# Second attention of a four-stage transformer kernel: sixteen units of two batches, with the sum of the fused halves carried in SBUF

## The chip, the cores and the metric

The kernel runs on one core of a Trainium2 chip. The metric is the device time of one execution in microseconds (us); of several runs the median counts. The core has five engines with queues of their own: TensorE (PE, with its weight loads as PEld), VectorE (DVE), ScalarE (ACT), GpSimd (POOL) and SyncE (SP), which issues DMAs. Each runs its instructions in order and waits on semaphores for the others.

## The reference

Four blocks follow one another on x, of 16 batches, 100 tokens and 256 channels: a cross attention, a mixture of experts, a second cross attention whose linear layers are rounded to integers, and a recurrent cell. The change is in the third block:

```python
vis = bitnet_linear(dinov2_features, W_d2v, b_d2v)
image_embeds = bitnet_linear(vis, W_img, b_img)
fused = bitnet_linear(text_embeddings, W_txt, b_txt)
for Wa, ba in ((W_att0, b_att0), (W_att1, b_att1)):
    kv = bitnet_linear(image_embeds, Wa, ba)
    k = jnp.concatenate([kv, kv], axis=-1)
    scores = jnp.einsum('bse,bpe->bsp', fused, k) * inv_sqrt_e
    attn = jax.nn.softmax(scores, axis=-1)
    fused = fused + 0.1 * jnp.einsum('bsp,bpe->bse', attn, k)
avg_img = jnp.mean(image_embeds, axis=1, keepdims=True)
concatenated = jnp.concatenate([fused, jnp.broadcast_to(avg_img, (b, s, e))], axis=-1)
h = jax.nn.relu(bitnet_linear(concatenated, W_f1, b_f1))
```

`bitnet_linear` divides its input by the maximum of the whole tensor over 127, rounds it, and multiplies by weights of -1, 0 and 1. So the maximum over all of `concatenated` must be known before F1 starts. `kv` has 128 channels, and since k is kv twice, a score needs only the sum of the two 128-channel halves of `fused`. The image has 361 places (KV) in a batch.

## The kernel before

The stage lies between the text product, whose eight results ScalarE writes to `fused` (L1891), and the maximum over `fused` (L1983, L1487) on which the scale of F1 hangs. There are four passes over four batches each (Q = 4), and in each pass two layers r, so eight rounds. `att_tensor`, `att_scalar` and `att_vector` write the rounds out for each engine. TensorE does in a round, for all four batches in turn: keys (L1632) and values (L1637), scores (L1644), transposes of the probabilities (L1649), and attention by values (L1655). Each of these takes float32 operands but the first two. ScalarE evicts the keys (L1669), takes exponentials (L1673) and copies the transposed probabilities (L1677). VectorE evicts the values (L1688), adds the two halves of `fused` into `f12` (L1693), takes the negated scores with their minimum (L1696), the reciprocals (L1700) and the divisions of the probabilities (L1702), and adds a tenth of the result to both halves of `fused` (L1707). Once in a pass it takes the maximum over the four batches before (L1711).

Banks: batch q has bank q for keys, scores and result, and bank 4+q for values and transposes. A round's keys wait for the update of the round before, batch by batch. The first and last pass are written out, the other two are a loop.

Image roundings (L1586 on ScalarE, L1590 on VectorE) prepare two halves of `img_q`, one batch an instruction: all sixteen are done ahead of the attention, VectorE's odd ones while the text product runs and ScalarE's last four behind the text evictions. GpSimd adds f2's bias to x in four instructions (L1792) once the normalised x is taken; before and after that stand its reductions over partitions (L1492). Behind them it makes the cell's weights (L2161), which wait for the cell's loads (issued by SyncE after the last update) and for the scaled inputs of F1, of which VectorE's L1991 writes the last.

Of the kernel before, what the change touches and what calls it, by code (L numbers as in the profile page):

```python
# [10 lines left out]
ALU = mybir.AluOpType  # L11
ACT = mybir.ActivationFunctionType
AX = mybir.AxisListType
# [23 lines left out]
LG = 4  # L37
# [11 lines left out]
def build(nc, a, out):  # L49
    ctx = ExitStack()  # L50
    with ctx:
# [1567 lines left out]

        def att_tensor(pe):  # L1620
            def body(t, *_):
                first = isinstance(t, int) and t == 0
                for r in range(2):
                    n = 8 * t + 4 * r
                    for q in range(Q):
                        b = 4 * t + q
                        if first and r == 0 and q == 0:
                            pe.wait_ge(c_p1, B // 2 + B + B // 4)
                            pe.wait_ge(c_q, B // 2 + B // 4)
                        wait(pe, n_u, n + q - 3)  # L1630
                        for k in range(CC):
                            i = pe.matmul(bank[q][:, 0:KV], w_q[ATT + r][:, k, :],  # L1632
                                          img_q[:, k, bass.ds(b * KV, KV)], start=(k == 0), stop=(k == 1))
                        i.then_inc(n_k, 1)
                        for j in range(KJ):
                            for k in range(CC):
                                i = pe.matmul(bank[4 + q][0:KT, j * 128:(j + 1) * 128],  # L1637
                                              img_q[:, k, bass.ds(b * KV + j * KT, KT)], w_q[ATT + r][:, k, :],
                                              start=(j == 0 and k == 0), stop=(k == 1), skip_group_check=True)
                        i.then_inc(n_v, 1)  # L1640
                    for q in range(Q):
                        pe.wait_ge(n_ke, n + q + 1)
                        pe.wait_ge(n_f, n + q + 1)
                        pe.matmul(bank[q][0:T, 0:KV], f12[q], kvT[q], start=True, stop=True).then_inc(n_s, 1)  # L1644
                    for q in range(Q):
                        pe.wait_ge(n_ve, n + q + 1)
                        pe.wait_ge(n_p, n + q + 1)
                        for j in range(KJ):
                            i = pe.transpose(bank[4 + q][0:KT, j * T:(j + 1) * T],  # L1649
                                             prob[q][:, j * KT:(j + 1) * KT], ident[0:T, 0:T])  # L1650
                        i.then_inc(n_t, 1)
                    for q in range(Q):
                        pe.wait_ge(n_pte, n + q + 1)
                        for j in range(KJ):
                            i = pe.matmul(bank[q][:, 0:T], kvt[q][:, j, :], probT[q][:, j, :],  # L1655
                                          start=(j == 0), stop=(j == KJ - 1))
                        i.then_inc(n_o, 1)
                if first:
                    pe.wait_ge(c_p1, 2 * B)
                    pe.wait_ge(c_q, B)  # L1660
            run(pe, B // Q, 1, 0, 1, body)

        def att_scalar(s):
            def body(t, *_):
                for r in range(2):
                    n = 8 * t + 4 * r
                    for q in range(Q):
                        s.wait_ge(n_k, n + q + 1)
# [978 lines left out]
```

## Time and profile before

| | |
|---|---|
| median of 3 runs | 997.46 us (996.68 to 1001.53) |
| profiled execution | 992.82 us, of which the span of the core is 991.0 us |
| PE busy | 821.7 us (83%) |
| DVE busy | 725.7 us (73%) |
| ACT busy | 556.1 us (56%) |
| POOL busy | 292.6 us (30%) |
| chain that ended last, by engine | PE 54%, DVE 24%, issue 8%, ACT 7% |
| second attention | 745.5 to 854.6 us of the span |

The profile is a record of one execution. Its timeline lists instructions with start and duration, merged where the same instruction repeats; its groups give the number, the busy time and the mean of one; what stands in brackets or behind the last bar is the idle time of the engine just before, and what ended it. A matmul's recorded duration contains the drain of the array, so in a row of matmuls the starts tell the pace. PEclk is the clock granted to TensorE, 1.00 for 2.4 GHz and 0.50 for 1.2 GHz.

### The profile page before, as it was taken

The page shows a single profiled execution, that of the slowest core. Times are in us where ns is not written, and L with a number is a line of the kernel's source. Part 1 is how long each engine was busy: PE and PEld are TensorE (multiplying, and loading weights), DVE is VectorE, ACT ScalarE, POOL GpSimd, SP SyncE. Part 2 cuts the span into 40 slices and gives each one's busy share as a digit, 9 for nine tenths or more (in the row PEclk, how much of TensorE's full clock was granted, in tenths as well). Part 3 has the DMA queues.
Part 4 walks back from the last instruction along what each step waited for, and adds up shares of the span by engine and source line. Part 5 has one row for each costly group of instructions (what it writes and reads, how often), then busy time and mean ns, then how long its engine had stood idle before and what let it go on. Part 6 is the DMA issues. An engine that isn't in the chain of part 4 may idle for free.

```text
span 991.0 us, 22346 instructions
## 1 busy us (share of the span) xinstructions
PE 821.7 (83%) x8198; PEld 604.3 (61%) x8198; DVE 725.7 (73%) x1496; ACT 556.1 (56%) x1147; POOL 292.6 (30%) x238
## 2 busy tenths in 40 slices
PE   3777888988898777798899999986647888769995
PEld 2345666666666554587666777772125777549994
DVE  7568787787877898767566776636995666776865
ACT  3446666666665436433555556538975555573542
POOL 3336444353441515040421110007603000053400
PEclk9978999999999777999999999995557888889998
DMA  6423443334453346323275555534200000200002
GB/s 182 106 67 75 97 105 91 100 105 111 121 115 81 82 167 225 110 57 115 74 200 163 163 166 167 142 102 120 71 10 0 2 0 0 85 0 2 3 1 67
DMA packets 76991, 90.47 MB, mean 91 GB/s; under 512 B 22166, under 2 KB 64945, under 8 KB 76842
## 3 DMA queue, kind: packets, MB, share of 16 engines
q1 hardware_dynamic: 69562, 80.95, 29.6%
q0 software_dynamic: 6144, 7.42, 2.8%
q10 hardware_dynamic: 1216, 1.18, 0.4%
q8 instruction: 43, 0.70, 0.3%
q14 instruction: 26, 0.21, 0.1%
HBM read 73.86 MB, written 15.43 MB: 90 GB/s over the span
## 4 chain that ended last, share of the span: by engine, by line
PE 54%; DVE 24%; issue 8%; ACT 7%; DMA 3%; POOL 2%; SPq 1%; ACTq 0%; DVEq 0%; POOLq 0%
PE ps L1151 11%; PE ps L1138 8%; PE ps L337 4%; PE ps L527 4%; PE ps L425 3%; PE ps L1655 3%; PE ps L499 3%; DVE p L515 3%; PE ps L569 3%; DVE m L485 2%; PE ps L2099 2%; PE ps L480 2%; PE ps L1649 2%; PE ps L2110 1%; DVE pmax L1616 1%
## 5 line engine op out<-in xcount | busy, mean ns | idle before, releaser
L485 DVE TENSOR_REDUCE m<-ps 100x2 f32<-100x722 f32 x128 | 115.2, 903 | 52.9 <-PE ps L480 51.3
L506 ACT ACTIVATE p<-ps 128x800 f32<-128x800 f32 x128 | 106.8, 835 | 43.0 <-PE ps L499 40.0
L1200 ACT ACTIVATE hT<-ps,cols 128x500 f32<-128x500 f32 (+1 forms) x96 | 62.5, 651 | 106.4 <-PE ps L1138 98.3
L1151 PE MATMUL ps<-w_h,hT_h 128*125 128x256 f16 (+1 forms) x384 | 105.9, 276 | 7.4 <-DVE x L1247 6.8
L515 DVE SCALAR_TENSOR_TENSOR p<-p 128x600 f32<-128x600 f32 x128 | 107.0, 838 | 0.0
L1207 DVE TENSOR_TENSOR hT_l<-hT,hT_h 128x500 f16<-128x500 f32 (+1 forms) x96 | 62.3, 652 | 60.9 <-ACT hT_h L1201 60.9
L1151 PE MATMUL ps<-w_h,hT_l 128*125 128x256 f16 (+1 forms) x384 | 105.9, 276 | 0.0
L1151 PE MATMUL ps<-w_l,hT_h 128*125 128x256 f16 (+1 forms) x384 | 105.8, 276 | 0.0
L1043 POOL DMA_INDIRECT xe<-tokens,slot_of x32 | 43.1, 1347 | 155.4 <-PE ps L1161 102.1
L1138 PE MATMUL ps<-xe_h,w_h 128*128 128x500 f16 (+1 forms) x192 | 71.7, 374 | 14.3 <-ACT hT_h L1201 6.1
L499 PE MATMUL ps<-qs,ks 128*128 128x100 f16 x768 | 64.7, 215 | 14.3 <-ACT p L506 14.3
L1138 PE MATMUL ps<-xe_l,w_h 128*128 128x500 f16 (+1 forms) x192 | 71.2, 371 | 0.0
L1138 PE MATMUL ps<-xe_h,w_l 128*128 128x500 f16 (+1 forms) x192 | 71.0, 370 | 0.0
L499 PEld LDWEIGHTS ps<-qs,ks 128*128 128x128 f16 x768 | 52.5, 101 | 28.5 <-ACT p L506 20.0
L355 POOL TENSOR_TENSOR kp<-k,kp 128x361 f16<-128x361 f32 x32 | 31.3, 977 | 118.5 <-ACT kp L351 118.5
L480 PE MATMUL ps<-ks,qs 128*100 128x361 f16 x256 | 63.0, 332 | 1.6 <-DVE xnT L168 1.4
L1201 ACT ACTIVATE hT_h<-ps,cols 128x500 f16<-128x500 f32 (+1 forms) x96 | 62.1, 647 | 0.0
L1492 POOL PARTITION_ALL_REDUCE gmax<-cmax x6 | 2.2, 365 | 196.4 <-DVE cmax L1487 190.5
L1151 PEld LDWEIGHTS ps<-w_h,hT_h 128*125 128x125 f16 (+1 forms) x384 | 51.5, 134 | 12.3 <-DVE x L1247 6.0
L527 PE MATMUL ps<-p,v 128*32 128x100 f32 (+1 forms) x1536 | 48.0, 259 | 8.8 <-DVE p L515 8.6
L1151 PEld LDWEIGHTS ps<-w_l,hT_h 128*125 128x125 f16 (+1 forms) x384 | 51.6, 134 | 2.6
L1151 PEld LDWEIGHTS ps<-w_h,hT_l 128*125 128x125 f16 (+1 forms) x384 | 51.6, 134 | 0.0
(342 smaller groups left out, 2209.4 us busy)
## 6 DMA issues: line engine op xcount, KB each, us to landing
sw<-in_L_ffn_w_dram SPq DMA_DIRECT2D x16, 512.0 KB, 6.3
sw<-in_L_ffn_w_dram SPq DMA_DIRECT2D x8, 1024.0 KB, 5.9
k_parts<-kp SPq DMA_DIRECT2D x32, 192.0 KB, 2.0
ks<-k_parts SPq DMA_DIRECT2D x32, 192.0 KB
stage<-in_L_xattn_W_f_dram SPq DMA_DIRECT2D x6, 1024.0 KB, 7.4
ctx_f<-in_ctxT_dram SPq DMA_DIRECT2D x16, 270.8 KB, 3.1
stage<-in_ctxT_dram SPq DMA_DIRECT2D x8, 541.5 KB, 8.6
area<-in_ctxT_dram SPq DMA_DIRECT2D x16, 270.8 KB, 6.2
```

What stands on the lines that cost most here:

```text
L480: mm = pe.matmul(bank[at + n][0:T, 0:KV], qs[p][:, h, :], ks[p][:, h, 0:KV], start=True, stop=True)
L485: v.tensor_reduce(m32[p][:, 2 * i:2 * i + 2], ps[0:T, at:at + 2, 0:KV], AX.X, ALU.max).then_inc(m_max, 1)
L499: mm = pe.matmul(bank[t_bank(i) + n][:, j * T:(j + 1) * T], keys, qs[p][:, h, :], start=(j == 0), stop=True, skip_group_check=True)
L506: s.activation(p32[:, i % HALF, :, :, :].rearrange("p j n t -> p n j t"), ps[:, t_bank(i):t_bank(i) + 2, 0:(KJ + 1) * T].rearrange("p n (j ...
L515: v.scalar_tensor_tensor(probs, probs, 1.0, low, ALU.min, ALU.max).then_inc(a_cv, 1)
L527: i = pe.matmul(OB_[HR * r:HR * (r + 1), g * T:(g + 1) * T], v32[p][0:m, j, h, :], p32[0:m, h // 2 % HALF, j, h % 2, :], start=(g == 0 and ...
L1043: g.indirect_dma_start(xe[e % 2][:, j, :], None, x_d, bass.IndirectOffsetOnAxis(ap=slot_of[:, 4 * e + j:4 * e + j + 1], axis=0)).then_inc( ...
L1138: i = pe.matmul(bank[2 + f % 2][:, 0:width(n)], w1p[ww][:, k, f * 128:(f + 1) * 128], xep[p][xx][:, k, 0:width(n)], start=(k == 0 and ww = ...
L1151: i = pe.matmul(bank[4 + j % 3][0:m, 0:C], hTp[p][hh][:, f, j * m:(j + 1) * m], w2p[of][ww][:, f, :], start=(f == 0 and hh == ww), stop=(f ...
L1200: s.activation(hT[:, f % 3, 0:m], bank[2 + f % 2][:, 0:m], ACT.Silu, bias=bias, scale=1.0 / WS)
L1201: s.activation(hTp[p][0][:, f, 0:m], bank[2 + f % 2][:, 0:m], ACT.Silu, bias=bias, scale=1.0 / WS).then_inc(f_s, 1)
L1207: v.tensor_tensor(hTp[p][1][:, f, 0:m], hT[:, f % 3, 0:m], hTp[p][0][:, f, 0:m], ALU.subtract).then_inc(f_l, 1)
```

## The change

The eight rounds of four batches become sixteen units of two. Unit u belongs to a pair of batches and a layer: the units 0 to 3 are pair 0 layer 0, pair 1 layer 0, pair 0 layer 1, pair 1 layer 1, and so on with the next pairs. On TensorE the work of three units is interleaved: scores of u, result of u-1, values and keys of u+1, transposes of u. Keys and scores have banks 0 and 1, values 2 and 3, transposes 4 and 5, results 6 or 7 by turns, two batches in one. All units are written out, without a loop.

`f12` covers two batches. GpSimd adds the halves of `fused` for it (new function `att_gpsimd`), once for each pair; for the second layer VectorE adds two tenths of the first layer's result to it straight from PSUM, beside the update of `fused`. The four additions of f2's bias now stand behind every second of these additions. The image roundings of the batches 5 and up on VectorE, and 8 and up on ScalarE, are put behind given units. The maximum over `fused` is taken in three parts of four batches, one of two before the last update and one of two after; the one over the image's mean comes ahead of the attention.

```diff
-        f12 = [over_vis(128, T) for _ in range(Q)]
+        f12 = [over_vis(128, 2 * T) for _ in range(2)]
+        UNITS = B
+        ROUND_ACT = {2: 8, 4: 10, 6: 12, 8: 14}
+        ROUND_DVE = {0: 5, 1: 7, 3: 9, 4: 11, 6: 13, 8: 15}
...
+            keys_values(0)
+            for u in range(UNITS):
+                if unit_of(u)[1] == 0:
+                    pe.wait_ge(n_f, u // 4 * 2 + u % 2 + 1)
+                else:
+                    pe.wait_ge(n_u, u - 1)
+                for q in range(2):
+                    pe.wait_ge(n_ke, 2 * u + q + 1)
+                    pe.matmul(bank[q][0:T, 0:KV], f12[u % 2][:, q * T:(q + 1) * T], kvT[at_slot(u, q)],
+                              start=True, stop=True).then_inc(n_s, 1)
+                values_out(u - 1)
+                keys_values(u + 1)
+                for q in range(2):
+                    pe.wait_ge(n_p, 2 * u + q + 1)
+                    for j in range(KJ):
+                        i = pe.transpose(bank[4 + q][0:KT, j * T:(j + 1) * T],
+                                         prob[at_slot(u, q)][:, j * KT:(j + 1) * KT], ident[0:T, 0:T])
+                    i.then_inc(n_t, 1)
+            values_out(UNITS - 1)
...
+            for u in range(UNITS):
+                for q in range(2):
+                    at = at_slot(u, q)
+                    s.wait_ge(n_sc, 2 * u + q + 1)
+                    s.activation(prob[at][:, 0:KV], neg_s[at], ACT.Exp, scale=-1.0, bias=small[:, 0, at:at + 1],
+                                 accum_out=small[:, 1, at:at + 1]).then_inc(n_e, 1)
+                keys(u + 1)
...
+                if u in ROUND_ACT:
+                    round_scalar(s, IMG_, img_f, img_q, 128, ROUND_ACT[u])
...
+        def att_gpsimd(g):
+
+            g.wait_ge(h_ev, 8)
+            for pair in range(B // 2):
+                tok = pair_tokens(pair)
+                u = pair // 2 * 4 + pair % 2
+                wait(g, n_s, 2 * (u - 1))
+                g.tensor_tensor(f12[u % 2], fused[:, 0, tok], fused[:, 1, tok], ALU.add).then_inc(n_f, 1)
+                if pair % 2:
+                    x_b2_gpsimd(g, pair // 2)
...
+                v.wait_ge(n_o, u + 1)
+                if unit_of(u)[1] == 0:
+                    v.scalar_tensor_tensor(f12[u % 2], bank[6 + u % 2][:, 0:2 * T], 0.2, f12[u % 2], ALU.mult, ALU.add)
+                v.scalar_tensor_tensor(fused[:, :, tok], bank[6 + u % 2][:, None, 0:2 * T].broadcast_to((128, CC, 2 * T)),
+                                       0.1, fused[:, :, tok], ALU.mult, ALU.add).then_inc(n_u, 1)
...
+                normalise(u, 0)
+                update(u - 1)
+                normalise(u, 1)
+                values(u + 1)
+                if u in ROUND_DVE:
+                    round_vector(v, IMG_, img_f, img_q, 128, ROUND_DVE[u])
+                if u % 4 == 1 and u > 4:
+                    v.wait_ge(n_u, u - 1)
+                    fused_max(u // 4 - 1, u // 4 * 4 - 4, u // 4 * 4)
+            v.wait_ge(n_u, UNITS - 1)
+            fused_max(3, B - 4, B - 2)
+            update(UNITS - 1)
+            v.wait_ge(n_u, UNITS)
+            vs.inc(fused_max(5, B - 2, B))
```

TensorE before, the first round (area3 holds the rounded image, area2 all of the attention's tiles; L1632 keys, L1637 values, L1644 scores, L1649 transposes, L1655 result):

```order
L1632 MATMUL ps<-area3,wq_att0 128x361 [waits c_q,c_p1,h_ev]
L1632 MATMUL ps<-area3,wq_att0 128x361
L1637 MATMUL ps<-wq_att0,area3 121x128 x6
L1632 MATMUL ps<-area3,wq_att0 128x361 x2
...
L1644 MATMUL ps<-area2 100x361 [waits n_f,n_ke] x4
L1649 MATMUL ps<-const,area2 121x100 [waits n_p,n_ve]
L1649 MATMUL ps<-const,area2 121x100 x2
...
L1655 MATMUL ps<-area2 128x100 [waits n_pte]
L1655 MATMUL ps<-area2 128x100 x2
```

TensorE now, unit 1 (L1680 scores, L1667 result of unit 0, L1647 values and L1655 keys of unit 2, L1687 transposes):

```order
L1680 MATMUL ps<-area2 100x361 [waits n_ke,n_f]
L1680 MATMUL ps<-area2 100x361 [waits n_ke]
L1667 MATMUL ps<-area2 128x100 [waits n_pte,n_ve]
L1667 MATMUL ps<-area2 128x100 x2
...
L1647 MATMUL ps<-wq_att1,area3 121x128 [waits n_ve]
L1647 MATMUL ps<-wq_att1,area3 121x128 x5
...
L1655 MATMUL ps<-area3,wq_att1 128x361 [waits n_sc]
L1655 MATMUL ps<-area3,wq_att1 128x361
...
L1687 MATMUL ps<-const,area2 121x100 [waits n_p]
L1687 MATMUL ps<-const,area2 121x100 x2
```

Between scores and transposes there was nothing; now the result of one unit and the keys and values of another stand there.

VectorE before, the second round of the first pass (L1688 values, L1693 sum of the halves, L1696 negated scores, L1700 and L1702 reciprocal and division, L1707 update):

```order
L1688 SCALAR_TENSOR_TENSOR area2<-ps,oscale,att_b1 121x384 [waits n_v]
L1693 TENSOR_TENSOR area2<-fused 128x100 [waits n_u]
...
L1696 TENSOR_SCALAR area2<-ps 100x361 [waits n_s] x4
L1700 RECIPROCAL area2<-area2 100x1 [waits n_e]
L1702 TENSOR_SCALAR area2<-area2 100x361 [waits n_r]
...
L1707 SCALAR_TENSOR_TENSOR fused<-ps,fused 128x2x100 [waits n_o] x4
```

VectorE now, unit 5 and the start of what follows (L1768 negated scores, L1744 and L1746 reciprocal and division, L1755 the carried sum, L1756 update, L1735 values of the next unit):

```order
L1768 TENSOR_SCALAR area2<-ps 100x361 [waits n_s] x2
L1744 RECIPROCAL area2<-area2 100x1 [waits n_e]
L1746 TENSOR_SCALAR area2<-area2 100x361 [waits n_r]
L1755 SCALAR_TENSOR_TENSOR area2<-ps,area2 128x200 [waits n_o]
L1756 SCALAR_TENSOR_TENSOR fused<-ps,fused 128x2x200
L1744 RECIPROCAL area2<-area2 100x1 [waits n_e]
L1746 TENSOR_SCALAR area2<-area2 100x361 [waits n_r]
L1735 SCALAR_TENSOR_TENSOR area2<-ps,oscale,att_b1 121x384 [waits n_v] x2
```

The update of the unit before stands between the two divisions, and the value evictions behind them.

GpSimd before, between the reduction for the text's scale and the one for F1's:

```order
L1492 ISA gmax<-cmax 128x1 [waits q_max] x2
L1792 ISA
L1792 TENSOR_TENSOR x<-x,f_b 100x1024 [waits ln_xn,c_b_in]
L1792 TENSOR_TENSOR x<-x,f_b 100x1024 x3
L1492 ISA
L1492 ISA gmax<-cmax 128x1 [waits q_max]
```

and now (L1724 sum of the halves, L1862 f2's bias):

```order
L1496 ISA gmax<-cmax 128x1 [waits q_max] x2
L1724 ISA
L1724 TENSOR_TENSOR area<-fused 128x200 [waits h_ev]
L1724 TENSOR_TENSOR area<-fused 128x200
L1862 TENSOR_TENSOR x<-x,f_b 100x1024 [waits ln_xn,c_b_in]
L1724 TENSOR_TENSOR area<-fused 128x200 [waits n_s] x2
L1862 TENSOR_TENSOR x<-x,f_b 100x1024
L1724 TENSOR_TENSOR area<-fused 128x200 [waits n_s] x2
L1862 TENSOR_TENSOR x<-x,f_b 100x1024
```

The additions of the bias are no longer in one row: each is released by the scores that its neighbour L1724 waits for.

## Rows read from the trace of the kernel before

**Rows 1.** Busy time by stretch: whole stage, and a piece of it; PEclk granted.

```profile
core 0: us, PE busy (x) PEld busy (x) DVE busy (x) ACT busy (x) POOL busy (x), PEclk, DMA share, GB/s
745.50:854.60 109.10, 93.51 (x608) 75.19 (x608) 73.77 (x227) 61.36 (x137) 9.17 (x4) 0.86 0.00 0
...
757.20:765.00 7.80, 7.73 (x37) 7.74 (x38) 2.47 (x8) 2.14 (x6) 0.00 (x0) 0.50 0.00 0
```

**Rows 2.** Groups of the stage: busy us, mean ns of one | idle before, releaser.

```profile
L1688 DVE SCALAR_TENSOR_TENSOR area<-ps,oscale,att_b 121x384 f32<-121x384 f32 x32 | 19.6, 612 | 6.8 <-PE ps L1637 6.8
...
L1707 DVE SCALAR_TENSOR_TENSOR fused<-ps,fused 128x200 f32 (+1 forms) x32 | 11.7, 366 | 29.4 <-PE ps L1655 29.4
...
L1673 ACT ACTIVATION_READ_ACCUMULATOR area<-area 100x1 f32 x32 | 6.0, 186 | 0.0
...
L1711 DVE TENSOR_REDUCE pmax<-fused x3 | 2.9, 974 | 0.0
```

**Rows 3.** Timeline of a round at full clock: start us, duration us, engine, instruction.

```profile
791.38 0.47 PE L1632 MATMUL ps<-area,wq_att 128*128 x2
...
793.96 2.63 PE L1644 MATMUL ps<-area 128*100 128x361 f32 x8
...
795.55 0.53 DVE L1696 TENSOR_SCALAR_CACHE_REDUCE area<-ps 100x361 f32<-100x361 f32 x1
...
796.12 0.60 ACT L1673 ACTIVATE area<-area 100x361 f32<-100x361 f32 x1 [1.64 <-DVE area L1696]
...
797.36 0.16 DVE L1700 RECIPROCAL area<-area 100x1 f32<-100x1 f32 x1
797.55 0.41 DVE L1702 TENSOR_SCALAR area<-area 100x361 f32<-100x361 f32 x1
...
798.11 2.07 PE L1649 MATMUL ps<-const,area 100*121 100x100 f32 x12 [1.51 <-DVE area L1702]
...
798.68 1.95 ACT L1677 COPY area<-ps 121x300 f32<-121x300 f32 x4
...
800.02 2.84 PE L1655 MATMUL ps<-area 121*128 121x100 f32 x24
...
800.89 0.37 DVE L1707 SCALAR_TENSOR_TENSOR fused<-ps,fused 128x200 f32 x1 [1.39 <-PE ps L1655]
...
802.70 0.47 PE L1632 MATMUL ps<-area,wq_att 128*128 x2
```

**Rows 4.** Timeline: first keys of two rounds that follow one another.

```profile
764.92 0.81 PE L1632 MATMUL ps<-area,wq_att 128*128 128x361 f16 x2
...
779.84 0.81 PE L1632 MATMUL ps<-area,wq_att 128*128 x2
```

**Rows 5.** Timeline of the front of the stage, all engines.

```profile
739.68 3.12 DVE L1590 TENSOR_SCALAR area<-area,iinv 128x722 f16<-128x722 f32 x6
...
745.33 9.35 POOL L1792 TENSOR_TENSOR x<-x,f_b 100x1024 f32<-100x1024 f32 x4 [7.22 <-issue]
745.45 3.27 ACT L1586 ACTIVATE area<-area,iinv 128x722 f16<-128x722 f32 x4
...
745.62 0.48 PE L1632 MATMUL ps<-area,wq_att 128*128 128x361 f16 x2 [1.32 <-ACT fused L1891]
...
748.26 1.88 DVE L1693 TENSOR_TENSOR area<-fused 128x100 f32<-128x100 f32 x1
748.73 1.28 ACT L1669 ACT_TABLE_LOAD   x1
...
750.74 1.46 PE L1644 MATMUL ps<-area 128*100 128x361 f32 x4 [2.36 <-ACT area L1669]
```

**Rows 6.** Timeline behind the stage: what GpSimd's weights wait for, and they.

```profile
860.01 0.76 DVE L1991 TENSOR_SCALAR area<-avg,iinv 128x400 f16<-128x400 f32 x2
...
865.41 5.91 POOL L2161 TENSOR_SCALAR fused<-area 128x512 f16<-128x512 f32 x4 [9.00 <-issue]
```

**Rows 7.** Timeline: end of the stage, the maximum over all parts.

```profile
855.73 0.16 DVE L1487 TENSOR_REDUCE cmax<-pmax 128x1 f32<-128x5 f32 x1
```

**Rows 8.** Timeline of an earlier stretch: a cast beside GpSimd's additions.

```profile
370.73 15.40 POOL L1262 TENSOR_TENSOR x<-x,pick_more 100x1024 f32<-100x1024 f32 x4 [20.02 <-DVE pick_more L1349]
...
379.19 2.35 DVE L1056 CAST upper<-const 100x100 bf16<-100x100 f32 x1
```

More of the change, by code:

```diff
@@ L1617, in lin_max_vector @@
                             ).then_inc(c_pm, 1)
-        def att_tensor(pe):
[L1621 to L1630, printed above, removed]
-                        for k in range(CC):
[L1632 to L1661, printed above, removed]
@@ L1663, in att_scalar @@
-        def att_scalar(s):
[L1664 to L1668, printed above, removed]
-                        s.activation(kvT[q], bank[q][:, 0:KV], ACT.Identity, scale=oscale[:, ATT + r:ATT + r + 1],
-                                     bias=col(f"L1_xattn_b_att{r}")).then_inc(n_ke, 1)
-                    for q in range(Q):
-                        s.wait_ge(n_sc, n + q + 1)
-                        s.activation(prob[q][:, 0:KV], neg_s[q], ACT.Exp, scale=-1.0, bias=small[:, 0, q:q + 1],
-                                     accum_out=small[:, 1, q:q + 1]).then_inc(n_e, 1)
-                    for q in range(Q):
-                        s.wait_ge(n_t, n + q + 1)
-                        s.copy(probT[q], bank[4 + q][0:KT, 0:KJ * T].rearrange("p (j t) -> p j t", j=KJ)
-                               ).then_inc(n_pte, 1)
-            run(s, B // Q, 0, 0, 1, body)
@@ new lines, in att_scalar, with keys @@
+        def att_scalar(s):
+            def keys(u):
+                if u == UNITS:
+                    return
+                r = unit_of(u)[1]
+                for q in range(2):
+                    s.wait_ge(n_k, 2 * u + q + 1)
+                    s.activation(kvT[at_slot(u, q)], bank[q][:, 0:KV], ACT.Identity,
+                                 scale=oscale[:, ATT + r:ATT + r + 1], bias=col(f"L1_xattn_b_att{r}")).then_inc(n_ke, 1)
+            keys(0)
+            for u in range(UNITS):
+                for q in range(2):
+                    at = at_slot(u, q)
[3 more added lines that the diff above has]
+                keys(u + 1)
+                for q in range(2):
+                    s.wait_ge(n_t, 2 * u + q + 1)
+                    s.copy(probT[at_slot(u, q)], bank[4 + q][0:KT, 0:KJ * T].rearrange("p (j t) -> p j t", j=KJ)
+                           ).then_inc(n_pte, 1)
+                if u in ROUND_ACT:
+                    round_scalar(s, IMG_, img_f, img_q, 128, ROUND_ACT[u])
@@ L1784, in y2_vector, with x_b2_gpsimd @@
                                        oscale[0:T, F2:F2 + 1], x[:, b:b + 2, :], ALU.mult, ALU.add).then_inc(y_ev, 2)
[L1786 to L1792 removed]
+        def x_b2_gpsimd(g, n):
+            if n == 0:
+                g.wait_ge(c_b_in, 48)
+                g.wait_ge(ln_xn, 3 * B)
+            part = x[:, LB * n:LB * (n + 1), :]
+            g.tensor_tensor(part, part, f2_b[:, None, :].broadcast_to((T, LB, C)), ALU.add).then_inc(x_bias, 1)
         def last_stats(v, g):
@@ L1893, in layer2_scalar @@
                              ).then_inc(h_ev, 1)
-            for b in range(B // 2, B, 2):
-                round_scalar(s, IMG_, img_f, img_q, 128, b)
             s.wait_ge(pad_set, 1)
@@ L1971, in layer2_vector @@
                                 ).then_inc(h_q2, 1)
-            for b in range(5, B, 2):
-                round_vector(v, IMG_, img_f, img_q, 128, b)
             for q in range(Q):
```

119 lines of the change are left out of this document (75 added, 44 removed).

## Prediction, made before the changed kernel was run

> **What bounds the kernel now.** Read first the table of stretches: the second attention runs from 745.5 to 854.6 us, and TensorE is busy in 93.5 of these 109.1 us, at a granted clock of 0.86 of full; inside it lie pieces at 0.50 [rows 1]. Then the timeline of one round at full clock, from 791.38 to 802.70, 11.3 us for four batches of one layer [rows 3]. TensorE does keys and values until 793.96, scores until 796.6, and then stands idle for 1.5 us, until 798.11, because the transposes want the normalised probabilities; before that VectorE took the four negated scores, ScalarE the exponentials, and VectorE the first division. From 798.11 it is busy to the end of the round, and VectorE waits (29.4 us over the stage for the last products of attention by values) [rows 2]. So the stage is TensorE's matmuls, plus one wait of softmax in each of eight rounds, plus what the clock loses after such waits: the round from 764.92 to 779.84 took 14.9 us, and its pair of key matmuls shows 0.81 us where the full clock has 0.47 [rows 3, 4].
>
> **TensorE's work for one batch and layer at full clock**, by starts [rows 3]: keys and values (793.96-791.38)/4 = 0.645; scores 2.63 less 0.16 of drain, over 4 = 0.62; transposes (800.02-798.11)/4 = 0.48; values out (802.70-800.02)/4 = 0.67. Together 2.41, or 4.83 us for a unit of two batches. Nothing of this is removed by the change.
>
> **Does the rest fit into 4.83 us?** I lay one unit from the start of its scores at 0. TensorE: scores to 1.24, values out of the unit before to 2.58, values and keys of the next to 3.87, transposes of its two batches at 3.87 and 4.35, next scores at 4.83. VectorE and ScalarE, with 0.2 us from a matmul's slot to its reader (the products that start at 800.02 have their first update at 800.89, that is 0.67+0.20), 0.57 from negated score to exponential (795.55 to 796.12), 0.58 and 0.19 for the exponential and its sum, 0.19 from reciprocal to division (797.36 to 797.55), 0.56 from division to transpose (to 798.11) [rows 2, 3]: the first batch's division starts at 2.44 and its transpose could start at 3.0, 0.9 early. The second batch's exponential ends at 2.8, but the update of the unit before stands ahead of its division in VectorE's queue, and waits for the values out at 2.78. This update now covers 400 elements for two batches: 0.37 us plus 200 elements at 0.98 a ns (800 took 0.97) is 0.57, near the 2x0.37 it replaces [rows 2, 3]. It ends at 3.4, and at 3.7 where the carried sum is updated as well. The second transpose is then ready at 4.15 or 4.46, against its slot at 4.35. So in units that follow a first-layer unit TensorE loses about 0.1: five such not counted elsewhere, 0.5 us. VectorE ends its two value evictions (0.61 each, less overlap) at 5.1 to 5.4 and is wanted at 5.7. ScalarE has two evictions, two exponentials and two copies, 3.6 us of work. Six image roundings of 0.52 us on VectorE and four of 0.82 on ScalarE go into the queues [rows 5]; ScalarE has 0.4 to spare and the first transpose 0.9, so I take 0.3 us for all ten, and 3 us if no slack were there.
>
> **Front of the stage.** Before, ScalarE first did four image roundings and a table load until 750.01, and the first score matmul stood at 750.74 [rows 5]. The roundings now come later and the load behind the first key evictions. The keys of unit 0 start two value groups after 745.62, at 746.3; they are evicted from 746.8, and scores start at 747.5: 3.2 us earlier. The fill of unit 0 is 4.55 us (no values out to do, but the table load of 1.28 now stands ahead of its exponentials), so unit 1 scores at 752.05.
>
> **End of the stage.** Unit 15 starts its scores 14x4.83 = 67.6 us later, at 819.7. From there by the slots above: second transpose 4.15, copy 4.72 to 5.13, values out to 6.0, update 6.2 to 6.8, and a maximum over 400 elements instead of 800, to 7.4. That is 827.1, without stalls; before, this point was 855.73, where the last maximum ends [rows 7]. Behind it nothing changes, and the weights' loads and the matmuls that follow hang on the same point.
>
> **What the moved work costs on GpSimd's side.** The sum of the two fused halves was 32 additions on VectorE, 0.25 us each. The change makes eight of them for two batches on GpSimd, and eight updates from PSUM on VectorE. The additions of f2's bias, four of 2.36 us, ran in one row at the start; there VectorE's addition with two inputs in SBUF took 1.88 us instead of 0.25, ending with GpSimd's instruction [rows 5]. Now three of the four start in units 3, 7 and 11, at about 2.1 us of the unit (scores ready 1.4, the addition about 0.6), and last until 4.45. VectorE's division, one input in SBUF and output in SBUF, comes at 2.44. Is it held too? A cast of 100 elements, also with one input, took 2.35 us beside a GpSimd addition [rows 8]. So I take that it is held: division until 4.8, update to 5.3, second division at 5.5, transpose at 6.0 instead of 4.35, 1.65 each and 5.0 us for three; the bounds are 0 and 3x2.4 = 7.1. The page "SBUF — State Buffer" of the Trainium skill, section "Who interferes with whom", says that only a VectorE instruction in a two-port mode or with two SBUF inputs is blocked for the whole of GpSimd's instruction, and names the scalar form with accumulator and reductions among the free ones. By it all hangs on whether the division is in such a mode; with it 977 below stands, without it the time would be 972. The trace leans to the mode: 361 elements in 0.41 us, against 800 in 0.97 for the reduction [rows 2, 3].
>
> **Maxima.** Three reductions of 0.97 us go into units 5, 9 and 13, behind the value evictions. VectorE then ends at 6.3 where 5.7 is wanted, and by the same slots the second transpose of the next unit is 0.65 late: 2.0 us for three.
>
> **Sum.** 827.1 + 0.5 + 0.3 + 5.0 + 2.0 = 834.9, against 855.7: 20.8 us less. The profiled execution took 992.8 us (span 991.0); from the median of 997.46, 4.6 above it, I take the same 20.8 off: 976.7, call it 977.
>
> **Rivals.**
> A. *No holding.* The division isn't held, and slots close without loss: 5.0 and 2.8 us back, 969. For it: evictions that read PSUM (L1688) aren't stretched beside GpSimd. Against it: rows 8.
> B. *The clock still falls.* A wait in a unit, 1.65 us where GpSimd holds, is as long as the idle 1.5 us of a round now, after some of which the clock fell and after others not. A round with a fall costs 14.9-11.3 = 3.6 us more [rows 3, 4]. One to three falls: 980 to 988.
> C. *GpSimd's first addition comes late.* GpSimd stood 7.22 us between a reduction over partitions and its first ordinary instruction [rows 5], and the new first addition feeds the first scores. If that change of program began only after the wait for the text evictions (745.6), the scores would start at 753.4: 5.9 later, 983. Against it: after the next such change its instruction ran at 865.41, only 4.7 us after what it waits for, which ends at 860.8 [rows 6]. So the change runs ahead of the wait.
> D. *Slower.* The pipeline keeps small waits in every unit and the clock stays at its half level through the stage. A unit then takes up to 9.6 us, 4.8 more. The gain is used up when five or so of sixteen units run so (20.8/4.8 = 4.3); all sixteen would give 1054. Against it: TensorE's share in the stage rises from 0.86 to about 0.93, and the rounds at full clock kept it at less.
> E. *The change doesn't pipeline.* A wait closes the ring and each unit runs alone: scores 1.24, softmax of the second batch to 3.6, a transpose 0.5, copy 1.0, values out 1.34, about 6.5 us a unit. Sixteen are 104 us from 747.5, an end near 852, and 994: within the noise. For it nothing: TensorE's row has the next unit's keys between scores and transposes, and no wait there is for the same unit's softmax.
>
> **Chances.** The forecast with its holding 0.52; A 0.13; B 0.22; C 0.06; D 0.03; E 0.04. Nearly all the mass is on one side. Range: 8 in 10 between A's end and B's, 969 to 988. A difference of 0.5% (5 us) is about what a measurement of this kernel can tell from none: faster 0.93, same 0.04, slower 0.03.
>
> **What would show it.** In the profile after: the first scores at about 747.5; sixteen units at 4.8 to 5.0 us, of which those with a GpSimd addition of 2.36 us are some 1.6 longer, with a division in them of over 1 us; granted clock near 1.00 from 750 to 825; the last maximum ending near 835. Wrong would be: divisions of 0.41 us everywhere (A), key matmul pairs of 0.81 us (B, D), a gap of 7 us before the first addition (C). The working is also wrong if the unit's length isn't TensorE's sum, because the queue of VectorE, whose slots I have only to some 0.3 us, sets it: 0.3 us in each of fourteen units would be 4 us.

## The result

| | kernel before | changed kernel |
|---|---|---|
| median | 997.07 us (4 runs) | 967.02 us (4 runs, 966.51 to 969.31) |
| ratio | | 0.9701, 95% interval 0.9671 to 0.9730 |
| profiled execution | 992.82 us, span 991.0 | 969.31 us, span 967.5 |
| a second comparison | 996.64 us (11 runs) | 968.04 us, ratio 0.9712 (0.9682 to 0.9743) |
| a third comparison | 989.32 us (17 runs) | 959.36 us, ratio 0.9696 (0.9676 to 0.9715) |
| second attention, first matmul to last maximum, three traces each | 110.1, 110.2, 109.9 us | 83.4, 83.4, 83.4 us |

The changed kernel is faster by about 30 us, or 3%. The forecast was 20 us, 977, with a range from 969 to 988: the time lies 2 us below its lower end. The mechanism is the one forecast; the stage was taken as 89.3 us (834.9 less 745.6), and is 83.4.

The table of stretches of the kernel after, as in [rows 1]: the stage, and the piece ahead of it.

```profile
core 0: us, PE busy (x) PEld busy (x) DVE busy (x) ACT busy (x) POOL busy (x), PEclk, DMA share, GB/s
...
739.00:747.50 8.50, 5.52 (x16) 2.26 (x16) 1.92 (x12) 7.16 (x10) 0.35 (x1) 0.51 0.01 2
...
747.50:830.90 83.40, 76.25 (x608) 61.00 (x608) 72.27 (x196) 54.42 (x134) 14.05 (x12) 1.00 0.00 1
```

TensorE has the same 608 matmuls as in [rows 1]. They are busy for 76 instead of 93 us, mostly since the granted clock is 1.00 where it was 0.86, and the stage is 7 us longer than that, where it was 16.6 longer. The front of the stage, timeline, to be held against [rows 5]:

```profile
747.56 0.89 PE L1647 MATMUL ps<-wq_att,area 128*121 128x128 f16 x12 [0.78 <-ACT fused L1961]
747.60 1.18 POOL L1724 TENSOR_TENSOR area<-fused 128x200 f32<-128x200 f32 x2 [7.82 <-ACT fused L1961]
...
748.85 1.20 ACT L1699 ACTIVATE area<-ps,cols,oscale 128x361 f32<-128x361 f32 x2 [1.35 <-PE ps L1655]
...
749.65 1.43 PE L1680 MATMUL ps<-area 128*100 128x361 f32 x4 [0.59 <-ACT area L1699]
...
750.06 1.28 ACT L1707 ACT_TABLE_LOAD   x1
```

The scores start 2.1 us after the first matmul, where [rows 5] have 5.1. GpSimd's first addition starts with the first matmul, so its change of program had run ahead of the wait, and rival C is out. Then one unit that TensorE sets, from its scores (L1680) by the result of the unit before (L1667), values (L1647), keys (L1655) and transposes (L1687) to the next scores:

```profile
789.32 1.38 PE L1680 MATMUL ps<-area 128*100 128x361 f32 x4
...
790.54 1.48 PE L1667 MATMUL ps<-area 121*128 121x100 f32 x12
...
791.86 0.84 PE L1647 MATMUL ps<-wq_att,area 128*121 128x128 f16 x12
...
792.53 0.78 PE L1655 MATMUL ps<-area,wq_att 128*128 128x361 f16 x4
...
793.15 0.78 PE L1687 MATMUL ps<-const,area 100*121 100x100 f32 x6
...
793.84 1.43 PE L1680 MATMUL ps<-area 128*100 128x361 f32 x4
```

No row has an idle time in brackets: 4.52 us without a gap, 1.22 + 1.32 + 0.67 + 0.62 + 0.69. The forecast had 4.83 here, with 0.96 for the transposes; from the first of them to the next scores it is 0.69. And a unit in which GpSimd adds f2's bias, the one before:

```profile
783.29 1.38 PE L1680 MATMUL ps<-area 128*100 128x361 f32 x4
...
785.33 2.35 POOL L1862 TENSOR_TENSOR x<-x,f_b 100x1024 f32<-100x1024 f32 x1
...
785.80 2.07 DVE L1746 TENSOR_SCALAR area<-area 100x361 f32<-100x361 f32 x1
...
787.93 0.56 PE L1687 MATMUL ps<-const,area 100*121 100x100 f32 x3 [0.65 <-DVE area L1746]
...
788.93 0.56 PE L1687 MATMUL ps<-const,area 100*121 100x100 f32 x3 [0.44 <-DVE area L1746]
```

It takes 6.03 us. The division that takes 0.41 us elsewhere takes 2.07, until GpSimd's addition has ended, and TensorE waits twice. The starts of the sixteen units' scores lie 4.06, 4.64, 4.64, 6.03, 4.52, 4.73, 5.02, 6.03, 4.52, 4.74, 5.02, 6.03, 4.51, 4.60 and 5.02 us apart. The end of the stage, as [rows 7]:

```profile
829.71 0.58 DVE L1756 SCALAR_TENSOR_TENSOR fused<-ps,fused 128x400 f32<-128x400 f32 x1 [1.65 <-PE ps L1667]
830.32 0.57 DVE L1760 TENSOR_REDUCE pmax<-fused 128x1 f32<-128x400 f32 x1
830.92 0.16 DVE L1491 TENSOR_REDUCE cmax<-pmax 128x1 f32<-128x6 f32 x1
```

And groups of the stage, as in [rows 2]:

```profile
L1746 DVE TENSOR_SCALAR area<-area 100x361 f32<-100x361 f32 x32 | 18.3, 572 | 1.1
L1687 PE MATMUL ps<-const,area 100*121 100x100 f32 x96 | 15.9, 282 | 5.3 <-DVE area L1746 5.2
...
L1756 DVE SCALAR_TENSOR_TENSOR fused<-ps,fused 128x400 f32<-128x400 f32 x16 | 9.1, 566 | 1.7 <-PE ps L1667 1.6
```

VectorE's 29.4 us of waiting for results in [rows 2] are 1.7 now; its mean division went from 408 to 572 ns, which is the holding.

### The profile page after: what moved, and what is told of

Same layout as the page of the kernel before. It is cut to its first block, busy times and chain, and to the rows that moved or that the text cites. A ratio compares the mean times of both kernels' runs of the same rounds, so it can differ in the third digit from the quotient of the medians.

```text
span 967.5 us, 22055 instructions
## 1 busy us (share of the span) xinstructions
PE 801.3 (83%) x8198; PEld 587.7 (61%) x8198; DVE 720.3 (74%) x1457; ACT 549.6 (57%) x1144; POOL 297.5 (31%) x246
## 4 chain that ended last, share of the span: by engine, by line
PE 50%; DVE 25%; ACT 12%; issue 8%; DMA 2%; SPq 1%; ACTq 0%; POOL 0%; DVEq 0%
PE ps L1151 11%; PE ps L1138 8%; PE ps L527 4%; PE ps L337 4%; PE ps L425 3%; PE ps L499 3%; PE ps L569 3%; DVE p L515 3%; DVE m L485 2%; ACT area L1615 2%; PE ps L480 2%; PE ps L2163 2%; PE ps L2174 1%; DVE area L1746 1%; ACT area L1590 1%
## 5 line engine op out<-in xcount | busy, mean ns | idle before, releaser
L499 PEld LDWEIGHTS ps<-qs,ks 128*128 128x128 f16 x768 | 52.2, 101 | 29.4 <-ACT p L506 20.1
L499 PE MATMUL ps<-qs,floor_k 128*128 128x100 f16 x256 | 51.4, 214 | 0.0
```

What stands on the lines that cost most here:

```text
L499: mm = pe.matmul(bank[t_bank(i) + n][:, j * T:(j + 1) * T], keys, qs[p][:, h, :], start=(j == 0), stop=True, skip_group_check=True)
```

## The experiments

Stage means from here on the time from the first key or value matmul to the start of the reduction over all maxima, in the trace. It repeats within 0.3 us, which the total doesn't: in all traces together the stage starts between 738.7 and 750.5 us of the span.

**The kernel before, again.** No edit.

> The kernel before, unchanged, for its spread and a second trace. Theory 1 (the number of rounds at half clock differs from run to run): the attention stage, from its first key matmul to the last maximum, differs from the 110.1 us of the first trace by multiples of about 3.6 us, with a granted clock away from 0.86, while the other stages agree within 1 or 2 us. Theory 2 (the spread of the time lies in other stages): this stage takes 110 us again within 1 us at 0.86.

Measured: median 993.09 us against 992.42 of the kernel before timed beside it, ratio 0.9996 (0.9975 to 1.0018). The stage took 110.2 us, with a granted clock of 0.85:

```profile
746.80:857.00 110.20, 95.18 (x608) 75.93 (x608) 74.73 (x229) 61.31 (x136) 8.93 (x4) 0.85 0.00 0
```

Theory 2 holds. The stage is steady; in each of the three traces of this kernel four of its eight rounds have a stretch at half clock, though not always the same four. The spread lies elsewhere.

**TensorE kept busy while it waits**, in the kernel before.

```diff
+                    pe.wait_ge(n_ve, n + 1)
+                    for _ in range(12):
+                        pe.matmul(bank[4][:, 384:512], w_q[ATT][:, 0, :], w_q[ATT][:, 1, :], start=True, stop=True,
+                                  skip_group_check=True)
                     for q in range(Q):
                         pe.wait_ge(n_ve, n + q + 1)
                         pe.wait_ge(n_p, n + q + 1)
```

> The kernel before with twelve 128-column matmuls on weights, whose result nobody reads, in each round between scores and transposes, where TensorE waits for softmax. If the lost clock is a cost of that idle time: granted clock of the stage near 1.00, no round over 12 us, the stage some 100 us instead of 110, ratio about 0.990. If the clock falls for another reason: clock 0.86 again, and the stage as long as before or a little longer.

Measured: median 985.76 us, ratio 0.9925 (0.9890 to 0.9960). The stage took 101.4 us at a granted clock of 0.95. The clock still fell once, after the long wait at the front that the filling doesn't reach: from first keys to first keys, the second round took 12.4 us, where [rows 4] have 14.9, and no later one over 11.5. The stage, and the filling (L1647) in a late round, which leaves 0.85 us of the wait of 1.5:

```profile
744.80:846.20 101.40, 90.23 (x704) 72.92 (x704) 74.85 (x229) 61.36 (x136) 8.69 (x4) 0.95 0.00 1
...
815.41 0.83 PE L1647 MATMUL ps<-wq_att 128*128 128x128 f16 x12
817.09 2.07 PE L1653 MATMUL ps<-const,area 100*121 100x100 f32 x12 [0.85 <-DVE area L1706]
```

Useless matmuls made the stage 8.7 us shorter, and the median 6.7. So at least 8.7 of the 26.8 us that the change gains there are the clock, which fell after TensorE had waited; how much the fall that is left at the front costs, no run shows. The rest is the waiting itself and the front.

**The pipeline taken out**, all else of the change kept.

```diff
-                values_out(u - 1)
-                keys_values(u + 1)
+                wait(pe, n_pte, 2 * u)
                 for q in range(2):
                     pe.wait_ge(n_p, 2 * u + q + 1)
...
                     i.then_inc(n_t, 1)
+                values_out(u - 1)
+                keys_values(u + 1)
...
                 normalise(u, 0)
-                update(u - 1)
                 normalise(u, 1)
+                update(u - 1)
```

> The changed kernel, where TensorE does the transposes of a unit right behind its scores, and the result of the unit before and keys and values of the next only then; VectorE does both divisions ahead of the update. All other parts of the change stay. Theory 1 (the gain is the cover of softmax by the neighbour units' matmuls): a wait of about 2.4 us comes back in each unit, 16 units are about 6.5 to 7 us each, the stage takes 110 to 118 us and the time is that of the kernel before or above, ratio 0.99 to 1.01. Rival (the gain is fewer instructions, GpSimd's sums and the written-out loop): the stage stays below 95 us, ratio below 0.98.

Measured: median 1019.16 us, ratio 1.0247 (1.0201 to 1.0292); the stage took 137.1 us. A unit takes 7.15 us at full clock, up to 9.9 where the clock fell, and 11.3 to 11.4 in the units 3, 7 and 11, where GpSimd's addition holds a division besides (2.0 to 2.3 us instead of 0.41). The stage, and a unit in which the clock fell:

```profile
745.16:882.29 137.13, 98.81 (x608) 73.33 (x608) 76.25 (x196) 53.91 (x133) 14.03 (x12) 0.85 0.00 1
...
754.06 1.86 PE L1680 MATMUL ps<-area 128*100 128x361 f32 x4 [0.23 <-ACT area L1700]
...
757.40 1.07 PE L1686 MATMUL ps<-const,area 100*121 100x100 f32 x6 [1.48 <-DVE area L1747]
...
758.31 2.73 PE L1667 MATMUL ps<-area 121*128 121x100 f32 x12
...
763.25 1.13 PE L1680 MATMUL ps<-area 128*100 128x361 f32 x3 [0.53 <-ACT area L1700]
```

The twelve result matmuls take 2.73 here and 1.48 in the pipeline, at 1.00. The order of TensorE's work is thus worth 53.7 us in this form, twice what the whole change brought (the edit moves VectorE's second division too, but that move alone, tried below, makes the stage shorter): units of two batches alone would be a loss, since they pay the wait for softmax sixteen times instead of eight. The mechanism of theory 1 holds, while its size (110 to 118 us) left out the clock and the holding.

**GpSimd's long additions cut.**

```diff
-            part = x[:, LB * n:LB * (n + 1), :]
-            g.tensor_tensor(part, part, f2_b[:, None, :].broadcast_to((T, LB, C)), ALU.add).then_inc(x_bias, 1)
+            part = x[:, LB * n:LB * (n + 1), 0:2]
+            g.tensor_tensor(part, part, f2_b[:, None, 0:2].broadcast_to((T, LB, 2)), ALU.add).then_inc(x_bias, 1)
```

> The changed kernel with GpSimd's four additions of f2's bias cut to 2 of 256 columns (the bias of most columns is left out). Theory 1 (a division of VectorE is held by them in three units): the three divisions of 2.1 to 2.3 us become 0.41, units 3, 7 and 11 take 4.6 instead of 6.03 us, and the stage is 4 to 4.5 us shorter, about 79; ratio lower by 0.0045 against the changed kernel. Rival (those units are long for another reason, the roundings): they stay near 6 us.

Measured: median 962.50 us, ratio 0.9690 (0.9653 to 0.9726) against the kernel before; the stage took 79.0 us. Units 3, 7 and 11 take 4.52 us each. The divisions, least, median and largest in ns:

```profile
L1746 DVE TENSOR_SCALAR area<-area x32: 407/408/411, 751.6 to 822.1; 100x361 f32<-100x361 f32 x32
```

The holding is shown, and costs 4.4 us; the forecast had 5.0.

**The changed kernel, again.** No edit.

> The changed kernel, unchanged, timed again beside many runs of the kernel before, and for a second trace. Theory 1 (the stage is worth 26.8 us, and the 30 us between the first medians are partly the spread of four runs, since 20 later runs of the kernel before have a median of 992.4): the stage takes 83.4 us again within 0.3, the ratio is 0.972 to 0.975 and the difference 25 to 28 us. Rival (the change also shortens something outside the stage): the ratio stays at 0.970, and another stretch of the trace is shorter.

Measured: ratio 0.9712, 28.6 us between the medians, the stage 83.39 us. The stage repeats; the difference is just above what theory 1 allowed. The two last runs below take this up.

**The additions put between divisions.**

```diff
                 if pair % 2:
+                    wait(g, n_p, {0: 0, 1: 12, 2: 20, 3: 26}[pair // 2])
                     x_b2_gpsimd(g, pair // 2)
```

> The changed kernel, where the second to fourth of GpSimd's additions of f2's bias wait for the second division of unit 5, 9 and 12, so that they lie between the divisions of two units; nothing is left out. Cutting them to 2 columns made the stage 4.4 us shorter, 78.98. Theory 1 (only divisions and roundings on VectorE are held): 79 to 80 us, ratio lower by 0.004 than the changed kernel. Rival (GpSimd's addition costs VectorE wherever it lies): 82 to 83.4 us.

Measured: median 965.21 us, ratio 0.9684 (0.9645 to 0.9722); the stage took 79.0 us, the same as with the additions cut. One of them in the timeline, released by a division, 2.35 us long, with the next of GpSimd's behind it:

```profile
775.09 2.35 POOL L1863 TENSOR_TENSOR x<-x,f_b 100x1024 f32<-100x1024 f32 x1 [11.37 <-DVE area L1747]
777.40 0.61 POOL L1724 TENSOR_TENSOR area<-fused 128x200 f32<-128x200 f32 x1
```

What costs is only what VectorE wants to run at that time: neither the negated scores and value evictions, which read PSUM, nor the maxima beside it grew.

**Divisions ahead of the update.**

```diff
                 normalise(u, 0)
-                update(u - 1)
                 normalise(u, 1)
+                update(u - 1)
```

> The changed kernel, where VectorE does both divisions of a unit ahead of the update of the unit before. Theory 1 (VectorE's order, with the second division behind the update, makes units longer than TensorE's 4.5 us): the units of 4.7 and 5.0 us shrink towards 4.5, the stage is 1.5 to 3 us shorter, 80.5 to 82. Rival (the units that are long are so by the sum of VectorE's work, maxima included, or by GpSimd): the stage stays within 0.7 us of 83.4. The later update could also delay the next scores of a second layer, which wait for it: then longer.

Measured: median 965.88 us, ratio 0.9674 (0.9634 to 0.9714); the stage took 81.0 us, 2.3 less. Units 1 and 2 went from 4.64 to 4.51 and 4.57, the held ones from 6.03 to 5.6. There the update in the middle was what made the second transposes late. It isn't the cause in the units behind a maximum: units 6 and 10 took 5.02 and take 5.09 and 4.93. Of the 2.3 us, some 1.3 come from the three held units and 0.35 from the end.

**All roundings ahead again.** The two tables are emptied, and the two loops of the kernel before put back.

```diff
-        ROUND_ACT = {2: 8, 4: 10, 6: 12, 8: 14}
-        ROUND_DVE = {0: 5, 1: 7, 3: 9, 4: 11, 6: 13, 8: 15}
+        ROUND_ACT = {}
+        ROUND_DVE = {}
...
+            for b in range(B // 2, B, 2):
+                round_scalar(s, IMG_, img_f, img_q, 128, b)
             s.wait_ge(pad_set, 1)
             att_scalar(s)
...
+            for b in range(5, B, 2):
+                round_vector(v, IMG_, img_f, img_q, 128, b)
             for q in range(Q):
                 i = v.memset(prob[q][:, KV:KP], 0.0)
```

> The changed kernel with all ten image roundings ahead of the attention again, as in the kernel before. The prediction took 2.9 of its 3.2 us of earlier start for this move. Theory 1: the first scores come 3.2 us later after the first value matmul (5.3 instead of 2.1 us), the units with roundings get 0 to 0.3 us shorter each, the stage is 1 to 3 us longer, 84.5 to 86.5. Rival (the roundings cost as much inside the units as ahead): 83.4 again.

Measured: median 972.87 us, ratio 0.9741 (0.9701 to 0.9782); the stage took 85.5 us, 2.2 longer. The scores started 3.8 us after the first matmul instead of 2.1. Not all of the 2.2 us is the later start (1.7): unit 0 took 4.9 us instead of 4.1, at a granted clock of 0.65 where the changed kernel has 1.00 there:

```profile
753.69:758.60 4.91, 4.91 (x27) 3.44 (x27) 2.66 (x10) 3.86 (x8) 0.00 (x0) 0.65 0.00 0
```

TensorE had waited 2.27 us for the keys just before. The units 1 to 14 are together 0.4 us shorter without the roundings in them (6.05, 4.52 and 4.60 where they were 6.03, 4.52 and 4.73), so the roundings inside them are nearly free.

**Every transpose twice.**

```diff
-                    for j in range(KJ):
+                    for j in (0, 1, 2) * 2:
                         i = pe.transpose(bank[4 + q][0:KT, j * T:(j + 1) * T],
```

> The changed kernel, where TensorE does each transpose of the probabilities twice, into the same place. It prices what the prediction took at 0.48 us a batch. Theory 1 (TensorE's own pace is 0.31 us a batch; the 0.48 seen in the kernel before was VectorE's pace of one division in 0.52 us): six transposes take 1.2 us instead of 0.6, and units that TensorE sets go from 4.52 to 5.13; those set by VectorE (4.7, 5.0, 6.03) grow less; stage 90 to 93 us instead of 83.4. Rival (0.48 is TensorE's pace): units grow by 0.96, stage 96 us or more. Rival (VectorE sets all units): under 86 us.

Measured: median 975.67 us, ratio 0.9787 (0.9749 to 0.9825); the stage took 88.9 us, 5.5 more. Twelve transposes and the scores behind them:

```profile
820.54 1.41 PE L1687 MATMUL ps<-const,area 100*121 100x100 f32 x12
821.79 1.38 PE L1680 MATMUL ps<-area 128*100 128x361 f32 x4
```

That is 1.25 us for twelve, 0.104 each and 0.31 a batch: TensorE's own pace. All units without holding but the first take 5.07 or 5.08 now, with maximum or without. The stage grew by less than 16x0.6, and than theory 1 said: the units that were longer than 4.5 before had 0.1 to 0.5 us of room for TensorE.

**The sum added again.**

```diff
-                if unit_of(u)[1] == 0:
-                    v.scalar_tensor_tensor(f12[u % 2], bank[6 + u % 2][:, 0:2 * T], 0.2, f12[u % 2], ALU.mult, ALU.add)
-                v.scalar_tensor_tensor(fused[:, :, tok], ...).then_inc(n_u, 1)
+                first = unit_of(u)[1] == 0
+                i = v.scalar_tensor_tensor(fused[:, :, tok], ...)
+                if first:
+                    vs.inc(i)
+                    vs.sync(v)
+                    i = v.tensor_tensor(f12[u % 2], fused[:, 0, tok], fused[:, 1, tok], ALU.add)
+                i.then_inc(n_u, 1)
```

> The changed kernel, where VectorE doesn't carry the sum along from PSUM: after the update of fused for a first-layer unit it adds the two halves again, with a wait for its own write between. The carried sum is then worth the difference. Theory 1 (an addition from SBUF costs as much as the one from PSUM, 0.36 us, and the wait for its own write 0.1 to 0.3 more, in eight units): stage 0.5 to 3 us longer, 84 to 86.5. Rival (the carried sum is what makes the change): 88 us or more. An addition with two inputs in SBUF may besides be held by GpSimd's, once.

Measured: median 971.39 us, ratio 0.9745 (0.9700 to 0.9790); the stage took 84.5 us, 1.1 more. The units with this update grew by 0.13 each. The carried sum, which the title names, is worth 1.1 of the 26.8 us.

**Maxima one unit later.**

```diff
-                if u % 4 == 1 and u > 4:
+                if u % 4 == 2 and u > 4:
```

> The changed kernel, where the three maxima over four batches stand one unit later on VectorE, behind unit 6, 10 and 14 instead of 5, 9 and 13. The unit then delayed has an update of fused alone, without the carried sum. Theory 1 (the long units of 4.7 and 5.0 us are maxima and carried sum falling together): these shrink, and the stage is 0.7 to 1.5 us shorter, 82 to 82.7. Rival (a maximum costs its length less a fixed slack wherever it stands): within 0.3 of 83.4. Behind unit 14 it may also reach into the last unit and cost some 0.3 there.

Measured: median 968.75 us, ratio 0.9711 (0.9674 to 0.9748); the stage took 83.3 us, 0.1 less. The units of 5.02 became 4.55, 4.55 and 4.57: 1.4 us. But the stretch from the last scores to the end grew from 7.16 to 8.44 us. The maximum behind unit 14 delays the last softmax, which nothing covers: the last results start 4.75 us behind the last scores instead of 4.27. The other 0.8 us is the clock, which fell in this execution while the last results ran. Those results here, the stretch from the fall to the end (granted clock 0.50), and the same results in the changed kernel:

```profile
830.13 2.43 PE L1667 MATMUL ps<-area 121*128 121x100 f32 x12
...
830.50:833.82 3.32, 2.06 (x11) 1.81 (x9) 1.15 (x3) 0.24 (x1) 0.00 (x0) 0.50 0.00 0
...
828.03 1.64 PE L1667 MATMUL ps<-area 121*128 121x100 f32 x12
```

So theory 1 was right on the units. Its sum, 82 to 82.7, is met if one takes off the 0.8 us, an estimate from one trace; whether the clock falls there in every execution isn't shown.

**The three moves together.** The edits of the additions between divisions, divisions ahead of the update, and maxima one unit later.

> The three moves together: additions of f2's bias behind second divisions, both divisions ahead of the update, maxima one unit later. Nothing is left out. Alone, the first took 4.4 us off the stage and the second 2.4, of which some is the same (the held units go from 6.03 to 5.6 with the second). Theory 1 (TensorE's 4.52 us a unit is the floor): all units but the first at 4.5 to 4.6, stage 76.5 to 77.5 us, ratio against the kernel before 0.964 to 0.967. Rival (the moves overlap more): 78 to 79.

Measured: median 961.91 us, ratio 0.9656 (0.9622 to 0.9690) against the kernel before; the stage took 77.6 us:

```profile
746.00:823.60 77.60, 74.67 (x608) 61.03 (x608) 67.79 (x197) 53.50 (x133) 14.23 (x12) 1.00 0.00 1
```

The units behind the first are 4.5 to 4.6 us, but for one of 4.86, and TensorE is busy in 74.7 of 77.6 us. By the traces this is 5.8 us better than the changed kernel. By the times alone, 961.9 against 968.0 in two comparisons with the same 996.64 us for the kernel before, the two intervals still overlap.

**Both kernels once more.** No edits.

> The changed kernel, unchanged, with one more kernel of the same call being the kernel before, unchanged, so that some 6 to 12 runs of each stand beside 20 or so of the kernel before. Theory 1 (all of the gain is the stage's 26.8 us, the 28.6 and 30 us between medians so far are spread of runs): stage 83.4 us, difference between medians 25.5 to 28 us. Rival (the change takes some 2 to 3 us off somewhere outside the stage): 29 to 31 us again.

> The kernel before, unchanged, for a third trace. Stage 110.1 us; the stretch ahead of it ends between 744 and 748 us, that behind it takes 135 to 138 us, both as in the changed kernel, if nothing outside the stage differs. If the change gains outside it, one of the two is longer than in all traces of the changed kernel (742.8 to 747.6, and 136.3 to 136.6).

Measured: 959.36 us (5 runs) against 989.32 (17 runs), 30.0 us, ratio 0.9696 (0.9676 to 0.9715); the kernel before as one of the two gave 1.0011 (0.9991 to 1.0030). The stages took 83.4 and 109.9 us. Here theory 1 fails on the times: 30 us, not 28 at most. Yet the rival finds no place in the traces. Ahead of the stage, the three traces of the kernel before have 745.6, 746.9 and 743.6 us, and those of the changed kernel 747.6, 742.8 and 738.7; but its near copies, with the same instructions there, have up to 750.5. Behind the stage it is 135.3, 137.8 and 137.6 against 136.6, 136.3 and 136.0.

## Why the prediction was right or wrong

- **What bounds.** Right: TensorE with a wait for softmax in each round, and a clock that fell after such waits. The pipeline is worth 53.7 us in the new form, and keeping TensorE busy was worth 8.7 us in the old one. That the clock would hold at 1.00 was right.
- **TensorE's work for a batch, the term that failed.** "transposes (800.02-798.11)/4 = 0.48" was read as TensorE's pace. But in that round the divisions came one in 0.51 us, and each batch's transposes started with its division. [rows 3] merge TensorE's twelve rows to one of 2.07 us, in which this isn't to be seen. The divisions behind the first, and the first transpose of each batch, taken one by one from the trace of the kernel before:

```profile
798.07 0.41 DVE L1702 TENSOR_SCALAR area<-area 100x361 f32<-100x361 f32 x1
798.58 0.41 DVE L1702 TENSOR_SCALAR area<-area 100x361 f32<-100x361 f32 x1
799.10 0.41 DVE L1702 TENSOR_SCALAR area<-area 100x361 f32<-100x361 f32 x1
...
798.11 0.32 PE L1649 MATMUL ps<-const,area 100*121 100x100 f32 x1 [1.51 <-DVE area L1702]
...
798.62 0.32 PE L1649 MATMUL ps<-const,area 100*121 100x100 f32 x1
...
799.14 0.32 PE L1649 MATMUL ps<-const,area 100*121 100x100 f32 x1
...
799.65 0.32 PE L1649 MATMUL ps<-const,area 100*121 100x100 f32 x1
```

TensorE's own pace is 0.31, shown by doing each transpose twice. A unit is 4.51 to 4.52 us instead of 4.83 (0.27 of this is the transposes, 0.69 instead of 0.96), which over fourteen units is 4.4 of the 5.9 us that the stage was taken too long. This term alone doesn't take the time out of the range: with 4.4 us off, the forecast would have been 972.
- **Front.** Predicted 1.9 us from first matmul to scores, measured 2.1. The fill of unit 0 was put at 4.55, without a working, and took 4.06, 0.5 less. Why is open: TensorE's pace isn't it, as the two batches' transposes start 0.58 us apart there, each with its division.
- **Holding by GpSimd.** 5.0 predicted, 4.4 measured, shown by cutting and by moving the additions. The rule of the Trainium skill's page "SBUF — State Buffer", section "Who interferes with whom", agrees with the trace, as the division with one input and its output in SBUF was held for the rest of GpSimd's addition (2.07 us instead of 0.41), and what reads PSUM or reduces was not (0.53, 0.61 and 0.98 us beside the moved additions, as elsewhere). That the division runs in a two-port mode, on which the rule hangs, is inferred: in [rows 3] it takes 0.41 us, while the negated scores of as many elements, read from PSUM, take 0.53. The trace of before had let it be read from the cast in [rows 8].
- **Other stalls.** 2.8 us predicted (maxima 2.0, updates 0.5, roundings 0.3). Over 4.51 us, the units without holding have 2.3 us together: 0.5 in each of three behind a maximum, 0.1 to 0.2 in five of the other eight. The size was nearly right. Both causes are shown, the maxima by moving them, and the update ahead of the second division, for the units 1 and 2, by moving the update.
- **End.** 7.4 predicted, 7.16 measured.
- **Median.** The prediction took its gain off the median of 997.46. With a stage of 83.4 us in it, it would have said 971. The remaining 3 to 4 us to 967 are not explained: three comparisons gave 30.0, 28.6 and 30.0 us between the medians, the stage accounts for 26.8 or 26.7, and no other stretch of the traces differs beyond its own spread of several us. Whether there is a small gain outside the stage stays open.
- **Rivals.** A (no holding) would have been at 969, near the measured time, and is wrong all the same: the holding was there, and another term was too large. B, C, D and E didn't come about. What E and B describe was seen in the kernel without the pipeline: units that run alone, of 7.15 us where E had 6.5, and a clock of 0.85 over the stage, which made it 2.5% slower than the kernel before. E's 104 us for sixteen became 137, since each was longer and since the clock and the holding come on top.
- **The range** was drawn from rivals, all of which but one made the kernel slower than the forecast. For a term of the sum itself, taken from rows in which TensorE may have been fed by another engine, it had no width downwards. The time came out below it by two things together, the stage's 5.9 us and the 3 to 4 us that are not explained.

## What to carry to other kernels

Where the matmuls of one engine are fed by another's results one by one, the distance of their starts is the feeder's pace; take an engine's own pace from a stretch in which nothing else can hold it, or allow for both. Smaller units pay only if each one's latency is covered by the neighbours' work: with the same units uncovered the kernel lost 2.5%, and covered it gained 3%. Put long GpSimd additions where VectorE has no SBUF-to-SBUF work waiting, by a semaphore of that very work: it cost one wait and gave back 4.4 us.

## What the runs showed of the hardware

- Twelve matmuls whose results nobody reads, put into TensorE's wait for softmax in each round, made the stage 8.7 us shorter: the granted clock of the stage went from 0.86 to 0.95, and where rounds from first keys to first keys took 13.8 to 14.9 us, the second took 12.4 and the later ones 11.3 to 11.5.
- A transpose of 100 by 121 float32 elements goes through TensorE in 0.104 us at full clock (twelve in 1.25 us).
- Four roundings on ScalarE and six on VectorE, 6.4 us of work in sum, cost 0.4 us inside the units 1 to 14. Put ahead, they made the stage 2.2 us longer, 0.8 of which fell in a unit with a granted clock of 0.65.
- The same stretch of code is reached at 738.7 to 750.5 us in different executions, while the stage itself repeats within 0.3 us: for a change of one stage, the stage's length in the trace tells apart what the total can't. (Where a trace shows a fall of the clock inside the stage, as with the maxima moved, its length has to be read with it.)
